# Merge steps of a two-layer graph network: two steps' chunks in one word, and products of 96 columns

## The chip, the cores and the metric

One core of a Trainium2 chip runs the kernel. The metric is device time in microseconds (us), the median of several runs of the whole program; lower is better. In the rows below PE is TensorE's matmul, PEld its weight load, DVE is VectorE, ACT is ScalarE, POOL is GpSimd and SP is SyncE, whose work here is to issue DMAs. A q behind an engine's name is its instruction queue.

## What is computed

The inputs are 100,000 nodes of 96 f32 features, 50,000 edges sorted by destination, with 32 features each, and the weights of two layers:

```python
def _egnn_conv(x, src, dst, edge_attr, W_msg, W_edge, W_root, b):
    msg = x[src] @ W_msg + edge_attr @ W_edge
    agg = segment_max(msg, dst, num_segments=x.shape[0])
    agg = where(isneginf(agg), 0.0, agg)
    return agg + x @ W_root + b
c1 = leaky_relu(_egnn_conv(X, ..., W1_msg, W1_edge, W1_root, b1))
c2 = leaky_relu(_egnn_conv(c1, ..., W2_msg, W2_edge, W2_root, b2))
return layernorm(x + c2)
```

## The kernel before, in words

The program runs four phases: an edge phase and a merge for each of the two layers (the merges are called A and B in the prediction).

**Edge phase** (98 groups of 512 edges). GpSimd gathers source rows (L397), TensorE turns them (L443), multiplies by the message and edge weights (L450), VectorE scans along the edges for the running maximum of each destination (L866), TensorE turns the result back (L460), and VectorE copies it into the tensor `hold` (L873): 391 chunks of 128 edges by 96 columns, which stay in SBUF. Beside this TensorE computes the root term x @ W_root + b of all nodes (L473, L482), which goes to DRAM. In the edge phase of layer 1 the tables of the merge are worked out from the destinations: TensorE counts (L499 to L508), and VectorE writes them in small pieces, one per edge group (L764 to L840). `piece_words` (L821 to L823) makes `step_words`, one 32-bit word per merge step, which holds the place of the step's chunk in `hold`. The one-hot matrices, which both merges use, are also written once to DRAM as bytes (L884 to L887, stores at L277).

**Merge** (L558 to L571). The nodes lie in 782 blocks of 128. A merge step adds what one chunk of edges gives to one block: a matmul of a one-hot matrix (128 edges to 128 nodes, the weights) with the chunk (the moving operand) into the block's slot in PSUM. Chunks and blocks are walked together, in 391 + 782 - 1 = 1172 steps. A step moves on either to the next chunk or to the next block, and which of the two is known only from the data. So TensorE's queue reads the words into registers (L554) and works out two addresses per step: of the chunk in `hold` (word times 4, plus a base) and of the slot in PSUM (word times BACK, plus a constant of the step, modulo the 16,384 bytes of a partition, plus a base). These register operations are packed into one instruction per step, which the rows list as FUSED_REGOPS. An f32 matmul is issued as two passes, each with its weight load.

Steps go in 147 batches of 8. Sixteen words (two batches) are loaded at a time. The loop of TensorE's queue:

```python
if k % 2 == 0:
    words = load_words(k * BATCH, min(2 * BATCH, TP - k * BATCH))
pe.wait_ge(made if layer == 0 else grown, k + 1)
for i in range(n):
    ...
    nc.tensor.matmul(...).then_inc(stepped[layer], 1)
```

The one-hots of a batch lie in one of two buffers (`onehot`, NS = 2). In merge A VectorE makes them (L914 to L919), waiting for the steps of the batch before last; in merge B GpSimd loads their bytes from DRAM (L412) and casts them to f32 in four pieces (L430). ScalarE copies finished blocks out of PSUM (L684), seeds freed slots with the root term (L670), and SyncE's queue stores results and loads root rows (L307 to L336). Where ScalarE may go on, it learns from counts of steps that it loads four at a time into registers, followed by one `max` per word (L708 to L715), two of them in the last load of a layer.

In merge B each table of 2048 nodes (49 tables) is finished as soon as its blocks are out: VectorE applies the leaky ReLU (L932), adds x (L935), takes the statistics of the layer norm (L937 to L951) and normalises part of the blocks (L955); ScalarE takes the root of the variance (L719) and normalises the rest (L725). ScalarE issues its copies, seeds, roots and normalisations in one written order (L691 to L706).

Of the kernel before, what the change touches and what calls it, by code (L numbers as in the profile page):

```python
# [5 lines left out]
F32 = mybir.dt.float32  # L6
BF16 = mybir.dt.bfloat16
I32 = mybir.dt.int32
U8 = mybir.dt.uint8
# [8 lines left out]
C = 4  # L18
# [8 lines left out]
RING = 8  # L27
NS = 2
# [9 lines left out]
TABLES_TAKE = 3  # L38


def gnn(nc, x, src, dst, edge_attr, weights, out):
# [27 lines left out]
    with ExitStack() as ctx:  # L69
        def sb(name, shape, dt):  # L70
            return ctx.enter_context(nc.sbuf_tensor(name, shape, dt))
# [21 lines left out]
        hold_all = sb("hold", [P, CH * D + P - D], F32)  # L93
        arena = sb("arena", [P, max(2 * UNIT_RING * UB * D + (EDGE_RING + 4) * GE + 2 * BATCH * P // 4, UNIT_RING * UB * D + 5 * RI * D)], F32)
        onehot = sb("onehot", [P, NS, BATCH, P], F32)
        keep = sb("keep", [P, EDGE_RING, GE], BF16)
        assert EDGE_RING == 4
# [9 lines left out]
        rows = sb("rows", [ROWS_ON + 1, TP], I32)  # L107
# [21 lines left out]
        ring_bytes = keep[:].rearrange("p i n -> p (i n)").bitcast(U8).rearrange("p (i n) -> p i n", n=BW)  # L129
# [6 lines left out]
        flat = hold_all[:]  # L136
# [3 lines left out]
        def scratch(n, dt=F32):  # L140
            free_at[0] -= n
            a = flat[:, free_at[0]:free_at[0] + n]
            return a if dt is F32 else a.bitcast(dt)
# [17 lines left out]
        place_row = scratch(TP)  # L161
        end_row, open_row, open_i = scratch(2 * NSB), scratch(NBATCH), scratch(NBATCH, I32)
# [10 lines left out]
        BACK = next(b for b in range(RING * C * SLOT) if (b * D + SLOT) % (RING * C * SLOT) == 0)  # L173
# [66 lines left out]
        def within(value, most):  # L240
            return nc.s_assert_within(value, 0, most, skip_runtime_bounds_check_because="a place in the merge, worked out on the chip from counts of chunks")
# [194 lines left out]
        def _(pe):  # L436
# [116 lines left out]
            def load_words(at, n):  # L553
                return nc.values_load_multi_w_load_instructions(  # L554
                    step_words[0:1, at:at + n], engines=[mybir.EngineType.PE], min_val=0, max_val=(CH - 1) * D,
                    skip_runtime_bounds_check_because="places in the merge, worked out on the chip from counts of chunks")[1]

            def merge(layer):  # L558
                for k in range(NBATCH):
                    n = min(BATCH, T - k * BATCH)  # L560
                    if k % 2 == 0:
                        words = load_words(k * BATCH, min(2 * BATCH, TP - k * BATCH))
                    if layer == 0:
                        pe.wait_ge(made, k + 1)
                    else:
                        pe.wait_ge(grown, k + 1)
                    for i in range(n):
                        word = words[k % 2 * BATCH + i]
                        chunk_at, place_at = word, within((word * BACK + (k * BATCH + i) * SLOT) % (RING * C * SLOT), (RING * C - 1) * SLOT)
                        nc.tensor.matmul(ps_bytes[:, bass.ds(place_at, SLOT)].bitcast(F32), onehot[:, k % NS, i, :], flat[:, bass.ds(chunk_at, P)],  # L570
                                         start=False, stop=True, skip_group_check=True).then_inc(stepped[layer], 1)  # L571
# [163 lines left out]
        def _(dve):  # L735
# [13 lines left out]
            def then(ins):  # L749

                link[0] += 1
                ins.then_inc(vec, 1)
                dve.wait_ge(vec, link[0])
# [67 lines left out]
            def piece_words():  # L821
                nc.vector.tensor_scalar(step_words, chunk_row[0:1, :], float(D), None, ALU.mult)
                then(nc.vector.tensor_tensor(place_row[0:1, :], steps_f[0:1, :], chunk_row[0:1, :], ALU.subtract))  # L823
# [168 lines left out]
```

## Time and profile before

| | |
|---|---|
| median of 3 runs | 1884.19 us |
| lowest and highest run | 1880.46 and 1887.78 us |
| profiled execution, span from first to last instruction | 1876.7 us |
| TensorE busy in matmuls | 1519.6 us (81%) |
| VectorE busy | 1313.2 us (70%) |
| ScalarE and GpSimd busy | 1080.4 and 1084.8 us (58% each) |
| mean granted TensorE clock | 0.950 |

The times are of the whole program on the device. The profile is of one execution; what lies before its first and after its last instruction is not in the span, and its own total is not listed apart from the runs. A share of busy time is a mean over phases with different limits, so the rows are best read phase by phase. The phases: edge phase 1 up to about 549 us, merge A from 549 to 871, edge phase 2 to 1382, merge B with the finishes to the end.

### The profile page before, as it was taken

Reading aid. Unit: us, or ns where it says so; the run is one execution under the profiler, and the core shown is the slowest. Engines: PE = TensorE matmul, PEld = TensorE weight load, DVE = VectorE, ACT = ScalarE, POOL = GpSimd, SP = SyncE. Lnnn points to the kernel's source line nnn. Section 1 sums busy time; section 2 is a strip of 40 time slices with the busy share of each in tenths; the row PEclk is TensorE's granted clock in tenths of the full one; section 3 lists DMA queues with packets and bytes.
Section 4 is the critical chain, followed back from the end, with each engine's and each line's share of the span. In section 5 each row is a group of like instructions: output and inputs, shape, how many; then the busy total and the mean of one; then the engine's idle time right before and its main releaser. Section 6 shows DMA issues by size and latency. Waiting matters only on the chain.

```text
span 1876.7 us, 37108 instructions
## 1 busy us (share of the span) xinstructions
PE 1519.6 (81%) x11422; PEld 1348.9 (72%) x11422; DVE 1313.2 (70%) x2383; ACT 1080.4 (58%) x2450; POOL 1084.8 (58%) x1454
## 2 busy tenths in 40 slices
PE   3998888988889888886889888988987767676763
PEld 3677777777778888885778777777777667666662
DVE  3677676777665555553667767677736899999998
ACT  2354444545443455553555555555535888888887
POOL 6777777767600000002777777777757787675663
PEclk9999999999999999998999999999998998988887
DMA  7779999999865777885788888888867899999996
GB/s 145 203 213 266 271 266 263 264 276 273 245 226 169 226 248 261 279 277 189 204 225 228 238 229 235 226 223 242 223 223 215 267 290 298 296 299 296 294 300 176
DMA packets 505022, 459.13 MB, mean 245 GB/s; under 512 B 348553, under 2 KB 412340, under 8 KB 504836
## 3 DMA queue, kind: packets, MB, share of 16 engines
q1 hardware_dynamic: 444118, 321.15, 59.9%
q0 software_dynamic: 30976, 57.72, 12.7%
q10 hardware_dynamic: 29742, 77.88, 10.6%
q8 instruction: 103, 1.69, 0.4%
q14 instruction: 83, 0.68, 0.1%
HBM read 283.25 MB, written 173.37 MB: 243 GB/s over the span
## 4 chain that ended last, share of the span: by engine, by line
PE 30%; DVE 25%; DMA 19%; POOL 15%; issue 9%; ACT 1%; SPq 1%; POOLq 0%; DVEq 0%; ACTq 0%
PE ps L570 18%; DMA onehot_bytes<-arena 14%; POOL arena L397 13%; DVE stats L937 6%; DVE arena L880 4%; DMA arena<-nodes,src_perm 4%; DVE arena L935 4%; DVE arena L932 4%; PE ps L482 4%; POOL onehot L430 2%; PE ps L450 2%; PE ps L473 2%; PE ps L443 2%; DVE arena L955 2%; DVE arena L866 1%
## 5 line engine op out<-in xcount | busy, mean ns | idle before, releaser
L570 PE MATMUL ps<-hold,onehot 128*128 x4688 | 612.7, 293 | 186.2 <-POOL onehot L430 139.5
L570 PEld LDWEIGHTS ps<-hold,onehot 128*128 128x128 f32 x4688 | 582.3, 205 | 217.0 <-issue 216.8
L397 POOL DMA_INDIRECT arena<-nodes,src_perm x392 | 370.0, 944 | 473.4 <-SPq L364 354.2
L482 PEld LDWEIGHTS ps<-w_root,onehot 97*128 97x128 f32 x3136 | 400.9, 194 | 99.7 <-issue 97.5
L397 POOL DMA_INDIRECT arena<-in_x_dram,src_all x392 | 374.4, 955 | 143.0 <-issue 114.3
L482 PE MATMUL ps<-w_root,onehot 97*128 97x128 f32 x3136 | 417.6, 277 | 0.0
L430 POOL CAST onehot<-keep 128x256 f32<-128x256 uint8 x588 | 298.8, 556 | 115.5 <-PE ps L570 72.4
L634 ACT COPY arena<-ps 128x384 f32<-128x384 f32 x392 | 187.5, 478 | 274.2 <-PE ps L482 272.4
L684 ACT COPY arena<-ps 128x384 f32<-128x384 f32 x392 | 166.6, 477 | 208.6 <-PE ps L570 208.5
L866 DVE TENSOR_TENSOR_SCAN arena<-keep,arena,ps 96x512 f32<-96x512 bf16 x196 | 247.7, 1264 | 46.6 <-PE ps L450 46.2
L880 DVE TENSOR_TENSOR onehot<-count,rel 128x1024 f32<-128x1024 bf16 x147 | 179.5, 1222 | 142.3 <-PE ps L570 141.2
L880 DVE TENSOR_TENSOR arena<-ps,rel 128x1024 uint8<-128x1024 f32 x147 | 175.5, 1216 | 110.6 <-DMA onehot_bytes<-arena 110.4
L473 PE MATMUL ps<-ident,arena 128*96 128x128 f32 x1568 | 240.9, 277 | 0.0
L725 ACT ACTIVATE arena<-arena,small 128x96 f32<-128x96 f32 x635 | 232.7, 454 | 1.6 <-DVE small L951 1.6
L450 PE MATMUL ps<-arena,w_edge 128*96 128x512 f32 x392 | 207.2, 611 | 0.0
L443 PE MATMUL ps<-ident,arena 128*128 128x128 f32 (+1 forms) x784 | 125.7, 284 | 96.2 <-DMA arena<-nodes,src_perm 63.7
L670 ACT COPY ps<-arena 128x384 f32<-128x384 f32 x392 | 175.9, 488 | 8.8 <-DMA arena<-root 8.3
L473 PEld LDWEIGHTS ps<-ident,arena 128*96 128x96 f32 x1568 | 177.2, 128 | 2.8 <-issue 2.4
L851 DVE TENSOR_TENSOR arena<-ps,arena 128x512 f32<-128x512 f32 x98 | 67.6, 690 | 146.9 <-ACT arena L613 144.5
L443 PEld LDWEIGHTS ps<-ident,arena 128*128 128x128 f32 (+1 forms) x784 | 93.2, 146 | 106.9 <-DMA arena<-nodes,src_perm 61.4
L624 ACT COPY onehot<-ps 96x512 f32<-96x512 f32 x196 | 114.3, 583 | 95.1 <-PE ps L473 92.4
L460 PE MATMUL ps<-ident,arena 96*128 96x96 f32 (+1 forms) x782 | 99.0, 249 | 52.8 <-DVE arena L880 51.8
(97 smaller groups left out, 1158.4 us busy)
## 6 DMA issues: line engine op xcount, KB each, us to landing
root<-arena ACTq DMA_DIRECT2D x196, 384.0 KB
arena<-root SPq DMA_DIRECT2D x196, 384.0 KB, 4.4
nodes<-arena SPq DMA_DIRECT2D x98, 384.0 KB, 2.7
arena<-nodes SPq DMA_DIRECT2D x98, 384.0 KB
arena<-in_x_dram SPq DMA_DIRECT2D x97, 384.0 KB
arena<-in_x_dram SPq DMA_DIRECT2D x48, 768.0 KB, 8.0
out_dram<-arena SPq DMA_DIRECT2D x48, 768.0 KB, 4.6
onehot_bytes<-arena SPq DMA_DIRECT2D x147, 128.0 KB
```

The source lines that it names most:

```text
L397: nc.gpsimd.indirect_dma_start(out=gathered[t.ring][0:t.p, i, 0:D], out_offset=None, in_=table_in, in_offset=bass.IndirectOffsetOnAxis(ap= ...
L430: last = nc.gpsimd.tensor_copy(onehot[:, k % NS, i:i + PIECE, :].rearrange("p t n -> p (t n)"), bytes_back(k, 1)[:, 0, i * P:(i + PIECE) * P])
L443: last = nc.tensor.transpose(et_ps[:, r:t.cols:C], gathered[t.ring][0:t.p, r, :], ident[0:t.p, 0:t.p])
L450: nc.tensor.matmul(em_ps[t.b2][0:D, 0:t.cols], w_edge[:, t.layer, :], edges_t[t.b2][:, 0:t.cols], start=True, stop=True).then_inc(em_full, 1)
L473: last = nc.tensor.transpose(nt_ps[m % 2][0:D, to], node_in[u % UNIT_RING][:, at:at + D], ident[:])
L482: last = nc.tensor.matmul(no_ps[m % 2][:, i * P:(i + 1) * P], nodes_t[m % NODE_RING][0:D + 1, i * P:(i + 1) * P], w_root[0:D + 1, layer * ...
L570: nc.tensor.matmul(ps_bytes[:, bass.ds(place_at, SLOT)].bitcast(F32), onehot[:, k % NS, i, :], flat[:, bass.ds(chunk_at, P)], start=False, ...
L634: nc.scalar.copy(root_out[u % UNIT_RING][:, at:at + C * D].rearrange("p (j d) -> p j d", d=D), no_ps[m % 2].rearrange("p (j k) -> p j k", ...
L670: nc.scalar.copy(slot[:, n % RING, :, 0:D], root_in[u % UNIT_RING][:, at:at + C * D].rearrange("p (j d) -> p j d", d=D),).then_inc(seeded[ ...
L725: last = nc.scalar.activation(nodes_out[s % 3][:, at], nodes_out[s % 3][:, at], ACT.Identity, bias=small[:, 5 + 2 * (s % 2), j:j + 1], sca ...
L866: nc.vector.tensor_tensor_scan(msgs[t.b2][0:D, at], keep[0:D, t.ring, at], em_ps[t.b2][0:D, at], msgs[1 - t.b2][0:D, GE - 1:GE], ALU.min, ...
L880: return nc.vector.tensor_tensor(to[:, 0:n, :], row.rearrange("p (a n) -> p a n", a=1).broadcast_to([P, n, P]), rel[:, k * BATCH:k * BATCH ...
```

## The change

The chunk index of a step, plus the distance of the step from the end of its round of 32 (`ahead`), takes ten bits. Two steps' values go into one 32-bit word, so that 16 loaded words serve 32 steps, and `load_words` runs every fourth batch (LOADED = 4). A step takes its half out of the word (`% SECOND` for even steps, `// SECOND` for odd ones), multiplies by the 384 bytes of a chunk and has the chunk's address; the slot follows from the same product (times BACK, now 84, modulo 16,384), with no constant of the step. For the chunk's address to hold `ahead`, the data before `hold` must belong to the same tensor: the buffers `onehot` and `keep` (together RING * C * D words per partition) now lie at its head. The product takes the 96 columns of the chunk in place of 128 (96 and 32 of what follows). `piece_words` has five VectorE operations in place of two. The number of steps, batches, buffers, semaphores, waits and DMAs is as before.

```diff
+SECOND = 1 << 10
+LOADED = 4
...
-        hold_all = sb("hold", [P, CH * D + P - D], F32)
+        AHEAD = RING * C * D
+        hold_all = sb("hold", [P, AHEAD + CH * D + P - D], F32)
...
-        onehot = sb("onehot", [P, NS, BATCH, P], F32)
-        keep = sb("keep", [P, EDGE_RING, GE], BF16)
-        assert EDGE_RING == 4
+        assert EDGE_RING == 4 and AHEAD == NS * BATCH * P + EDGE_RING * GE // 2
+        onehot = hold_all[:, 0:NS * BATCH * P].rearrange("p (s t n) -> p s t n", s=NS, n=P)
+        keep = hold_all[:, NS * BATCH * P:AHEAD].bitcast(BF16).rearrange("p (i n) -> p i n", n=GE)
...
-        rows = sb("rows", [ROWS_ON + 1, TP], I32)
+        rows = sb("rows", [ROWS_ON + 1, TP // 2], I32)
...
-        flat = hold_all[:]
+        flat = hold_all[:, AHEAD:]
...
+        ahead_i, ahead_row = scratch(TP, I32), scratch(TP)
...
-        BACK = next(b for b in range(RING * C * SLOT) if (b * D + SLOT) % (RING * C * SLOT) == 0)
+        hold_bytes, CHUNK = hold_all[:].bitcast(U8), 4 * D
+        BACK = next(b for b in range(RING * C * SLOT) if (b * CHUNK + SLOT) % (RING * C * SLOT) == 0)
+        assert CH + RING * C < SECOND and (CH + RING * C) * SECOND < 1 << 24 and T % 2 == 0 and BATCH % 2 == 0
+
+        def ahead(t):
+
+            return RING * C - t % (RING * C)
+
+        def chunk_view(t, word):
+
+            at, most = 4 * AHEAD - ahead(t) * CHUNK, (CH - 1 + ahead(t)) * CHUNK
+            return hold_bytes[:, at:at + most + CHUNK][:, bass.ds(within(word, most), CHUNK)].bitcast(F32)
...
                 for k in range(NBATCH):
                     n = min(BATCH, T - k * BATCH)
-                    if k % 2 == 0:
-                        words = load_words(k * BATCH, min(2 * BATCH, TP - k * BATCH))
+                    if k % LOADED == 0:
+                        words = load_words(k * BATCH // 2, min(LOADED * BATCH, TP - k * BATCH) // 2)
...
                     for i in range(n):
-                        word = words[k % 2 * BATCH + i]
-                        chunk_at, place_at = word, within((word * BACK + (k * BATCH + i) * SLOT) % (RING * C * SLOT), (RING * C - 1) * SLOT)
-                        nc.tensor.matmul(ps_bytes[:, bass.ds(place_at, SLOT)].bitcast(F32), onehot[:, k % NS, i, :], flat[:, bass.ds(chunk_at, P)],
+                        word = words[(k % LOADED * BATCH + i) // 2]
+                        chunk_at = pe.snap((word // SECOND if i % 2 else word % SECOND) * CHUNK)
+                        place_at = within(chunk_at * BACK % (RING * C * SLOT), (RING * C - 1) * SLOT)
+                        nc.tensor.matmul(ps_bytes[:, bass.ds(place_at, CHUNK)].bitcast(F32), onehot[:, k % NS, i, :], chunk_view(k * BATCH + i, chunk_at),
                                          start=False, stop=True, skip_group_check=True).then_inc(stepped[layer], 1)
...
             def piece_words():
-                nc.vector.tensor_scalar(step_words, chunk_row[0:1, :], float(D), None, ALU.mult)
-                then(nc.vector.tensor_tensor(place_row[0:1, :], steps_f[0:1, :], chunk_row[0:1, :], ALU.subtract))
+                pairs = lambda a: a[0:1, :].rearrange("a (t n) -> a t n", n=2)
+                nc.vector.tensor_tensor(place_row[0:1, :], steps_f[0:1, :], chunk_row[0:1, :], ALU.subtract)
+                then(nc.vector.tensor_scalar(ahead_i[0:1, :], steps_i[0:1, :], RING * C - 1, None, ALU.bitwise_and))
+                then(nc.vector.tensor_scalar(ahead_row[0:1, :], ahead_i[0:1, :], -1.0, float(RING * C), ALU.mult, ALU.add))
+                then(nc.vector.tensor_tensor(ahead_row[0:1, :], ahead_row[0:1, :], chunk_row[0:1, :], ALU.add))
+                nc.vector.scalar_tensor_tensor(step_words, pairs(ahead_row)[:, :, 1], float(SECOND), pairs(ahead_row)[:, :, 0], ALU.mult, ALU.add)
```

## Rows read from the trace of the kernel before

**Rows 1.** The page: span, and the chain that ended last, by line.

```profile
span 1876.7 us, 37108 instructions
...
PE ps L570 18%; DMA onehot_bytes<-arena 14%; POOL arena L397 13%; DVE stats L937 6%; DVE arena L880 4%; DMA arena<-nodes,src_perm 4%; DVE arena L935 4%; DVE arena L932 4%; PE ps L482 4%; POOL onehot L430 2%; PE ps L450 2%; PE ps L473 2%; PE ps L443 2%; DVE arena L955 2%; DVE arena L866 1%
```

**Rows 2.** By stage: length, busy us of PE, PEld, DVE, ACT, POOL; clock; DMA.

```profile
549.20:870.75 321.55, 282.36 (x2344) 268.81 (x2344) 178.09 (x146) 160.18 (x387) 0.00 (x0) 0.99 0.73 239
...
1487.00:1876.70 389.70, 251.25 (x1758) 238.33 (x1757) 356.33 (x1132) 338.01 (x917) 254.06 (x489) 0.86 0.95 282
```

**Rows 3.** Who waited for whom, 549 to 870 us: total us, times, longest.

```profile
ACT arena L684 <- PE ps L570: 158.0, 97, 9.2
DVE onehot L880 <- PE ps L570: 141.2, 145, 2.5
...
PE ps L570 <- issue: 39.0, 71, 1.2
...
PE ps L570 <- DVE onehot L880: 2.1, 1, 2.1
```

**Rows 4.** Merge matmuls 653 to 663 us (timeline); line views of L570 and L554.

```profile
653.42 3.83 PE L570 MATMUL ps<-hold,onehot 128*128 x32 [0.66 <-issue]
657.91 3.83 PE L570 MATMUL ps<-hold,onehot 128*128 x32 [0.65 <-issue]
...
653.42 2.05 PE L570 MATMUL ps<-hold,onehot 128*128 x16 [0.66 <-issue]
...
L570 PE MATMUL ps<-hold,onehot x24: 275/275/372, 653.4 to 656.1; 128*128 x24
L570 PEldq FUSED_REGOPS  x16: 102/103/103, 653.3 to 656.0; - x16
...
L554 PEldq TENSOR_LOAD <-rows x73: 862/1268/1870, 552.1 to 868.5; - x73
```

**Rows 5.** Busy time of L570 alone, from the second load of merge A on.

```profile
553.20:870.75 317.55, 278.39 (x2325) 264.84 (x2324) 1.00 0.73 237
```

**Rows 6.** Who waited for whom, 1382 to 1487 us.

```profile
DVE arena L932 <- ACT arena L684: 25.7, 1, 25.7
PE ps L570 <- POOL onehot L430: 25.3, 14, 3.5
```

**Rows 7.** Weight loads after a stall (L570), and transposes of 96 columns (L460).

```profile
653.42 0.30 PEld L570 LDWEIGHTS ps<-hold,onehot 128*128 128x128 f32 x2 [0.84 <-issue]
...
L570 PEld LDWEIGHTS ps<-hold,onehot x2: 186/188/189, 653.4 to 653.5; 128*128 128x128 f32 x2
...
1111.60 0.49 PE L460 MATMUL ps<-ident,arena 96*128 96x96 f32 x4
...
L460 PEld LDWEIGHTS ps<-ident,arena x4: 139/140/143, 1111.5 to 1111.8; 96*128 96x128 f32 x4
```

**Rows 8.** ScalarE's register instructions at L714: four operations, and the last with two.

```profile
L714 ACTq FUSED_REGOPS  x1: 55/55/55, 642.3 to 642.3; - x1
...
L714 ACTq FUSED_REGOPS  x1: 43/43/43, 867.1 to 867.1; - x1
```

**Rows 9.** VectorE's one-hots, 655 to 659 us (timeline).

```profile
655.58 1.22 DVE L880 TENSOR_TENSOR onehot<-count,rel 128x1024 f32<-128x1024 bf16 x1 [1.48 <-PE ps L570]
```

**Rows 10.** Busy time by stage, a stretch late in merge A.

```profile
820.00:840.00 20.00, 16.75 (x141) 15.82 (x140) 11.07 (x10) 11.82 (x29) 0.00 (x0) 1.00 0.88 280
```

**Rows 11.** GpSimd's casts, 1416 to 1426 us (timeline).

```profile
1419.21 1.43 POOL L430 CAST onehot<-keep 128x256 f32<-128x256 uint8 x4 [0.19 <-PE ps L570]
1420.86 4.33 POOL L430 CAST onehot<-keep 128x256 f32<-128x256 uint8 x4 [0.21 <-PE ps L570]
```

**Rows 12.** VectorE around the table of words, 98 to 106 us (timeline).

```profile
99.94 0.75 DVE L822 TENSOR_SCALAR rows<-hold 1x1176 int32<-1x1176 f32 x1
100.62 1.37 DVE L823 TENSOR_TENSOR hold<-hold 1x1176 f32<-1x1176 f32 x1
102.02 1.28 DVE L866 TENSOR_TENSOR_SCAN arena<-keep,arena,ps 96x512 f32<-96x512 bf16 x1
```

More of the change, by code:

```diff
@@ L128, in gnn @@
         BW = BATCH * P
-        ring_bytes = keep[:].rearrange("p i n -> p (i n)").bitcast(U8).rearrange("p (i n) -> p i n", n=BW)
+        ring_bytes = hold_all[:, NS * BATCH * P:AHEAD].bitcast(U8).rearrange("p (i n) -> p i n", n=BW)
         bytes_out = arena[:, at_rest + 4 * GE:at_rest + 4 * GE + 2 * BW // 4].bitcast(U8).rearrange("p (i n) -> p i n", n=BW)
@@ L554, in load_words @@
                 return nc.values_load_multi_w_load_instructions(
-                    step_words[0:1, at:at + n], engines=[mybir.EngineType.PE], min_val=0, max_val=(CH - 1) * D,
+                    step_words[0:1, at:at + n], engines=[mybir.EngineType.PE], min_val=0, max_val=(CH + RING * C) * SECOND - 1,
                     skip_runtime_bounds_check_because="places in the merge, worked out on the chip from counts of chunks")[1]
```

## Prediction

> **What bounds the kernel now.** I read the page first: the span and the chain that ended last, in which many lines share and the largest piece, 18%, is the line of the merge matmul [rows 1]. So the next view is the busy time by stage [rows 2]: the reader should see that the merge of layer 1 (merge A) is 321.6 us in which TensorE is busy 282.4, and that the end of merge B (from 1487 us) belongs to VectorE, busy 356 of 389.7. The change also touches, through a table, a few us of the first edge phase.
>
> In merge A ScalarE waits 158.0 us and VectorE 141.2 us for the matmuls, and TensorE has hardly a wait for them (2.1 us once) but 39.0 us of "issue" in 71 pieces [rows 3]. So TensorE and its own instruction queue bound it. One period shows how [rows 4]: 32 passes (16 steps of two passes each, since an f32 matmul goes as two) run in one burst of 3.83 us, and the next burst starts 4.49 us after the first. Between bursts the queue loads 16 words into registers; that load takes 1.27 us in the median. Inside a burst the first 16 passes take 2.05 us; the last of them lasts 0.275, and the first lasts 0.372 and not 0.275 because of the stall, so 15 distances make (2.05 − 0.275 − 0.097)/15 = 0.112 us a pass, 0.223 a step. The queue itself would be faster: its 16 register instructions start at 653.3 to 656.0, 2.7/15 = 0.18 us a step, of which the register instruction is 0.103.
>
> From this comes the price of one load. Over 317.55 us there are 2325 passes [rows 5]; 2325 × 0.1115 = 259.2 us, so 58.3 us are left for 73 loads: 0.80 us each. A load of 1.27 costs only 0.80 because the queue had run ahead. I count a load of 1.27 us plus 0.04 of restart, less the lead, so the mean lead was 0.51.
>
> Merge B is another matter: in its first 105 us, up to 1487, TensorE waits 25.3 us for GpSimd's casts, and VectorE's finishes wait 25.7 us for the first table of nodes [rows 6]. After that VectorE is busy almost without pause with the finishes [rows 2]: TensorE's speed there costs nothing.
>
> **The change, part by part.**
>
> *Fewer loads.* Words are now loaded every fourth batch, still 16 at a time: 37 loads a merge in place of 74. The duration of a load I leave at 1.27, since its 16 words are the same.
>
> *Narrower products.* Moving 96 columns for 128 would take a pass from 0.112 to 0.084 if columns alone counted. They don't: after a stall the first pass lasts 372 ns and not 275 [rows 4], 97 more, because it waits for its weights, and the two weight loads there are 0.30 − 0.189 = 0.11 us apart with nothing else in their way [rows 7]. That is the rate at which 128 f32 columns go in, and the change leaves the weights alone. Passes of 96 columns exist too: four take 0.49 us [rows 7], where four of 128 would take 3 × 0.112 + 0.275 = 0.61, so 0.03 less each, or 0.082 a pass. But those are transposes whose weight load lasts 139 to 143 ns, not 186 to 189, so they do not prove the faster rate here. I take 0.108 a pass, 0.216 a step, near the rate of the weight loads; the ends are 0.164 a step (columns alone) and 0.223 (nothing).
> By the Trainium skill (TensorE: Matmul & The Clock Gate, section "Back-to-back issue gap") the gap of isolated matmuls grows with the moving columns alone; it adds that in a stream the weight load counts as well. By the first half of that rule the sum would be that of the first rival below; the rows at the stall speak against it.
>
> *Register work of a step.* By the code a step needs six register operations now: two multiplications, three additions and a mod. Afterwards six: a division or a mod to take the chunk out of the word, two multiplications, a mod, two additions; the constant per step has moved into the word. So an addition becomes a second mod or a division. ScalarE's register instruction of four simple operations takes 55 ns and of two 43 [rows 8]: 6 ns an operation and 31 for the instruction. Six of those are 67, so 36 of the 103 belong to multiplying and to the mod. The new operation then adds 0 to 36 ns: the queue's step becomes 0.181 to 0.217. No row divides them further, so I take the middle, 0.199, and keep both ends.
>
> *The one-hots are late next.* Each batch of eight steps needs a one-hot made by VectorE in the buffer of the batch before last. The last pass of a batch started at 653.42 + 2.05 − 0.275 = 655.20; the one-hot started at 655.58 and took 1.22 [rows 4, 9]. With 0.04 to TensorE's queue, 0.15 of register and issue and 0.11 for the weights, the first product of the batch after next can start 1.90 us after that last pass. Today it is due 17 passes later, 1.90 us: just in time, and each load has hidden it. With passes of 0.108 it is due at 1.84, so it is 0.07 late once in four batches, and the queue loses its lead at the third and fourth batch. The lead at the next load is then what eight steps gain: 8 × (0.216 − 0.199) = 0.14.
>
> *Sum for merge A, per 32 steps.* Now 2 × (16 × 0.223 + 0.80) = 8.74 us. After: 32 × 0.216 + 0.07 + 1.31 − 0.14 = 8.15. Gain 0.59, times 1172/32 = 36.6: 21.5 us. With a queue step of 0.181 it is 26.6, with 0.217 (then the queue sets the step) 15.1, with passes unchanged 17.
>
> *Who else must keep pace.* ScalarE waits for the merge, not the merge for it [rows 3]. The DMA engines are 88% busy late in merge A [rows 10]; 7% more pace gives 94%. I add nothing.
>
> *Merge B.* In its first 105 us some 18 loads become 9, which by the above would free 9 × 0.8 = 7 us, but GpSimd is late next: four casts take 1.4 us when free and 4.3 beside VectorE's long operations [rows 11]. I take 4 us, between 0 and 7. After 1487 us nothing.
>
> *The table of words.* VectorE's two operations on 1176 elements (0.75 and 1.37 us) become five: the subtraction (1.37), a bit operation (some 0.75), a multiply-add (0.75), an addition (1.37), and a packing of half the length (0.7): 3 us more, estimated from the two rows. The scan behind them starts at 102.02, right when they end [rows 12], and the scans hold TensorE up, so nothing covers it: I take 3 us on the path, bounds 0 (if the edge phase catches up) and 3.1.
>
> *One tensor for two buffers and the waiting data.* No instruction is added or taken away and no wait changes; nothing is behind it that could be uncovered. Zero.
>
> Total: −21.5 − 4 + 3 = −22.5 us. The profiled execution has a span of 1876.7 us; the runs shown have a median of 1884.2, 7.5 above it, and I put the difference on that: **1862 us**. Its own range, with the ends of the queue's step, of merge B and of the table: 1852 to 1874.
>
> **The rivals.**
>
> *Columns alone count.* Passes fall to 0.082, the queue sets the step: 32 × 0.199 + 1.31 = 7.68, 38.7 us less in merge A, 6 in merge B, 3 for the table: 1842. For it: the transposes of 96 columns [rows 7]. Against it: the weight loads at the stall. Chance 0.13.
>
> *The register work eats the gain.* If the extraction costs more than any row here shows, the queue has no lead and sets the step: 32 s + 1.31 equals today's 8.74 at s = 0.232, a register instruction of 154 ns. At 0.225 merge A gains 8, merge B 1, less 3: 1878, no change that a measurement can tell. Chance 0.14.
>
> *Slower by the same place.* If a step's operations don't fit one instruction, a second one comes to it, which costs at least the 43 ns of the shortest and an issue of its own: s = 0.25. Then 32 × 0.25 + 1.31 = 9.31, 21 us more in merge A, 4 in merge B, 3 for the table: 1912. It decides from s = 0.232 upward. For it: 103 ns is already over half of the queue's step [rows 4], and its reserve to the step of TensorE is 0.04 us. Against it: the number of operations is the same. Chance 0.11.
>
> *The change does less than it says*: each load grows as its words serve more steps. The words per load are the same 16, so I give this 0.02, at 1876 to 1884.
>
> **How the numbers follow.** The forecast has 0.60. About 0.5% (9.4 us) is what a measurement of this kernel can tell from no change. Faster by more than that: the forecast and the first rival, less a tail: 0.73. Within it: 0.16. Slower: 0.11. The range from 1840 to 1884 takes in the first two rivals and leaves out the slower one and a little of the fast end.
>
> **What would show it.** In the changed profile: 37 loads of about 1.27 us a merge (74 in all); bursts of 64 passes with one gap of 1.0 to 1.2 us; passes 0.108 apart inside a burst (0.082 speaks for the first rival, 0.112 for no gain from columns); a register instruction of 103 to 139 ns, one per step (two per step or over 154 ns speaks for the slower rival); merge A some 300 us long in place of 321.6; the stage up to 549.2 about 3 us longer; VectorE still busy without a pause from about 1480 us. The forecast is wrong if merge A is shorter than 280 or longer than 312 us, or if its time comes back in the later stages.

## The result, and the profile after

| | before | after |
|---|---|---|
| median | 1883.70 us (4 runs) | 1910.18 us (4 runs) |
| lowest and highest run | 1880.46 and 1887.78 us | 1905.17 and 1913.95 us |
| profiled execution, span | 1876.7 us | 1906.2 us (its own time 1908.06 us) |

The ratio is 1.0144 with a 95% interval of 1.0110 to 1.0178: the change costs about 26 us. The forecast was 1862 us.

The page of the changed kernel: span, granted clock in 40 slices, chain that ended last by line ([rows 1] of before). The merge matmul is now L586, the cast L445, and the one-hots carry the name `hold`, since they lie in that tensor.

```profile
span 1906.2 us, 37037 instructions
...
PEclk9999999999999999888999999999987787887886
...
PE ps L586 23%; POOL arena L412 17%; DMA onehot_bytes<-arena 13%; POOL hold L445 7%; DVE arena L900 4%; DMA arena<-nodes,src_perm 3%; PE ps L497 3%; DVE stats L957 3%; DVE arena L955 2%; DVE arena L952 2%; PE ps L488 1%; DVE arena L886 1%; PE ps L465 1%; PE ps L458 1%; DMA hold<-onehot_bytes 1%
```

The merge matmul grew from 18% of the chain to 23%, and the clock line has 7 and 8 where merge B runs. By stage, with the stages cut at the first and the last product of each merge (columns as in [rows 2]; the seventh value is the granted clock): merge A, the first 100 us of merge B, and all of merge B.

```profile
552.70:885.30 332.60, 289.64 (x2344) 283.90 (x2344) 178.02 (x146) 159.89 (x386) 0.00 (x0) 0.94 0.70 231
1401.60:1501.60 100.00, 79.25 (x524) 76.04 (x524) 48.50 (x157) 48.60 (x127) 71.64 (x145) 0.81 0.72 220
1401.60:1885.50 483.90, 364.17 (x2343) 349.98 (x2344) 398.60 (x1268) 383.54 (x1035) 346.43 (x652) 0.81 0.91 273
```

The same cuts of the kernel before.

```profile
549.20:870.40 321.20, 282.02 (x2343) 268.67 (x2344) 178.09 (x146) 160.18 (x387) 0.00 (x0) 0.99 0.73 239
1382.10:1482.10 100.00, 75.65 (x561) 71.92 (x561) 55.34 (x169) 55.97 (x148) 76.63 (x153) 0.91 0.75 229
1382.10:1854.80 472.70, 330.02 (x2343) 313.37 (x2344) 400.46 (x1268) 382.32 (x1032) 334.58 (x652) 0.88 0.93 278
```

So the start of merge A is 3.5 us later, merge A 11.4 us longer, the edge phase of layer 2 4.6 us longer (885.3 to 1401.6 against 870.4 to 1382.1), merge B 11.2 us longer, and what follows the last product 1.2 us shorter. The granted clock has two levels in these records, 1.0 (2.4 GHz) and 0.5 (1.2 GHz), so a mean of g means that 2 × (1 − g) of the stretch was at 1.2 GHz. Added up from the single records of the clock, these are 38 us of merge A in place of 3, and 186 us of merge B in place of 110.

Inside merge A, first two bursts of the timeline ([rows 4] of before).

```profile
638.12 7.38 PE L586 MATMUL ps<-hold 128*128 x64 [0.91 <-issue]
646.59 7.44 PE L586 MATMUL ps<-hold 128*128 x64 [1.09 <-issue]
```

Then the line views (ns, shortest/median/longest): the loads of merge A, products and register instructions of both merges, and the register instructions that follow one load.

```profile
L569 PEldq TENSOR_LOAD <-rows x37: 950/1170/2746, 550.0 to 879.6; - x37
...
L586 PE MATMUL ps<-hold x4688: 274/276/525, 552.7 to 1885.5; 128*128 x196
L586 PEldq FUSED_REGOPS  x2344: 126/134/154, 552.5 to 1884.1; - x196
...
L586 PEldq FUSED_REGOPS  x7: 128/128/137, 646.4 to 647.7; - x7
```

Bursts of 64 passes with one load each, and one register instruction per step, as forecast. But a burst at full clock lasts 7.38 to 7.44 us: (7.4 − 0.275 − 0.1)/63 = 0.112 a pass, as before. And the register instruction takes 126 to 139 ns (one came to 154) in place of 103; while the queue runs freely, the starts of these instructions lie 0.209 and 0.217 us apart in turn, 0.213 a step in place of 0.181.

Who waited for whom in merge A ([rows 3] of before; us, times, longest).

```profile
ACT arena L700 <- PE ps L586: 170.4, 97, 10.4
DVE hold L900 <- PE ps L586: 141.5, 140, 4.1
...
PE ps L586 <- issue: 24.1, 24, 2.5
PE ps L586 <- DVE hold L900: 20.8, 13, 2.0
```

The two waits of TensorE sum to 44.9 us (before 41.1) although there are half as many: 37 of 1.2 us in place of 72 of 0.57. Thirteen of them now end with a one-hot.

And where the clock falls: two bursts of the timeline.

```profile
672.32 7.44 PE L586 MATMUL ps<-hold 128*128 x64 [1.18 <-issue]
681.16 9.08 PE L586 MATMUL ps<-hold 128*128 x64 [1.40 <-DVE hold L900]
```

The merge's own busy time in two stretches around the fall (PE, PEld, then the granted clock).

```profile
672.80:683.00 10.20, 8.80 (x78) 8.64 (x78) 1.00 0.71 233
683.00:686.40 3.40, 3.40 (x18) 3.40 (x18) 0.50 0.69 231
```

The second burst contains 3.4 us at 0.5, which 18 passes touch. In it 16 passes start, 0.213 us apart; at 0.112 there would have been 30. What TensorE did before the fall: a burst, a pause of 1.40 us, and 2 us of the next burst. Merge A has eight such falls, beside the one at its start which before has too.

### The profile page after: what moved, and what is told of

Same layout as the page of the kernel before. It is cut to its first block, busy times and chain, and to the rows that moved or that the text cites. A ratio compares the mean times of both kernels' runs of the same rounds, so it can differ in the third digit from the quotient of the medians.

```text
span 1906.2 us, 37037 instructions
## 1 busy us (share of the span) xinstructions
PE 1567.7 (82%) x11422; PEld 1407.4 (74%) x11422; DVE 1313.2 (69%) x2386; ACT 1081.2 (57%) x2450; POOL 1097.2 (58%) x1454
## 4 chain that ended last, share of the span: by engine, by line
PE 31%; POOL 24%; DMA 18%; DVE 15%; issue 10%; SPq 1%; ACT 1%; POOLq 0%; DVEq 0%; ACTq 0%
PE ps L586 23%; POOL arena L412 17%; DMA onehot_bytes<-arena 13%; POOL hold L445 7%; DVE arena L900 4%; DMA arena<-nodes,src_perm 3%; PE ps L497 3%; DVE stats L957 3%; DVE arena L955 2%; DVE arena L952 2%; PE ps L488 1%; DVE arena L886 1%; PE ps L465 1%; PE ps L458 1%; DMA hold<-onehot_bytes 1%
## 5 line engine op out<-in xcount | busy, mean ns | idle before, releaser
L586 PE MATMUL ps<-hold 128*128 x4688 | 654.4, 308 | 166.9 <-POOL hold L445 120.2
L586 PEld LDWEIGHTS ps<-hold 128*128 128x128 f32 x4688 | 634.1, 221 | 187.7 <-issue 186.6
L497 PEld LDWEIGHTS ps<-w_root,hold 97*128 97x128 f32 x3136 | 403.1, 195 | 99.8 <-issue 97.1
L497 PE MATMUL ps<-w_root,hold 97*128 97x128 f32 x3136 | 420.2, 278 | 0.0
L445 POOL CAST hold<-hold 128x256 f32<-128x256 uint8 x588 | 310.6, 575 | 114.9 <-PE ps L586 83.6
L900 DVE TENSOR_TENSOR hold<-count,rel 128x1024 f32<-128x1024 bf16 x147 | 179.5, 1222 | 154.2 <-PE ps L586 141.5
L886 DVE TENSOR_TENSOR_SCAN arena<-hold,arena,ps 96x512 f32<-96x512 bf16 x196 | 247.8, 1264 | 49.8 <-PE ps L465 49.5
L640 ACT COPY hold<-ps 96x512 f32<-96x512 f32 x196 | 114.2, 583 | 91.9 <-PE ps L488 85.2
```

The lines of the kernel that those rows point to most:

```text
L445: last = nc.gpsimd.tensor_copy(onehot[:, k % NS, i:i + PIECE, :].rearrange("p t n -> p (t n)"), bytes_back(k, 1)[:, 0, i * P:(i + PIECE) * P])
L497: last = nc.tensor.matmul(no_ps[m % 2][:, i * P:(i + 1) * P], nodes_t[m % NODE_RING][0:D + 1, i * P:(i + 1) * P], w_root[0:D + 1, layer * ...
L586: nc.tensor.matmul(ps_bytes[:, bass.ds(place_at, CHUNK)].bitcast(F32), onehot[:, k % NS, i, :], chunk_view(k * BATCH + i, chunk_at), start ...
L886: nc.vector.tensor_tensor_scan(msgs[t.b2][0:D, at], keep[0:D, t.ring, at], em_ps[t.b2][0:D, at], msgs[1 - t.b2][0:D, GE - 1:GE], ALU.min, ...
L900: return nc.vector.tensor_tensor(to[:, 0:n, :], row.rearrange("p (a n) -> p a n", a=1).broadcast_to([P, n, P]), rel[:, k * BATCH:k * BATCH ...
```

## The experiments

Each kernel ran beside runs of the kernel before on the same chip; a ratio is to those. Stage lengths are of one profiled execution. Single runs of the kernel before lay between 1870.6 and 1904.6 us, so a few us in one stage of one execution say little by themselves. This holds for merge B above all: the kernel before with halved one-hots, below, has no edit in merge B, and yet its merge B took 491.9 us at a granted 0.86 in the profiled execution, its longest run, where before has 472.7. Merge A of the same two took 320.9 and 321.2.

### The change cut in two

First the change with its old width: words packed, products of 128 columns.

```diff
-            return hold_bytes[:, at:at + most + CHUNK][:, bass.ds(within(word, most), CHUNK)].bitcast(F32)
+            return hold_bytes[:, at:at + most + SLOT][:, bass.ds(within(word, most), SLOT)].bitcast(F32)
...
-                        nc.tensor.matmul(ps_bytes[:, bass.ds(place_at, CHUNK)].bitcast(F32), onehot[:, k % NS, i, :], chunk_view(k * BATCH + i, chunk_at),
+                        nc.tensor.matmul(ps_bytes[:, bass.ds(place_at, SLOT)].bitcast(F32), onehot[:, k % NS, i, :], chunk_view(k * BATCH + i, chunk_at),
```

> The changed kernel with products of 128 columns again; packed words, register work and loads stay as changed. The changed kernel's batches at full clock are 16 us faster over merge A, but merge A has 34 us at the low clock where before had none after its start. Theory C (columns): narrower products leave TensorE less active, and with pauses that lowers its granted clock. Then the low clock goes from merge A, merge A takes 303 to 312 us (332.6 in the changed kernel, 321.2 before) and the total is 1868 to 1882. Theory G (gaps): the longer pause at each load (1.1 to 2.5 us where it was 0.5 to 1.2), since the queue has lost its lead, lowers the clock. Then the low clock stays, merge A takes 325 to 335 us and the total is 1903 to 1914.

Then the kernel before with nothing but the narrow product.

```diff
-                        nc.tensor.matmul(ps_bytes[:, bass.ds(place_at, SLOT)].bitcast(F32), onehot[:, k % NS, i, :], flat[:, bass.ds(chunk_at, P)],
+                        nc.tensor.matmul(ps_bytes[:, bass.ds(place_at, 4 * D)].bitcast(F32), onehot[:, k % NS, i, :], flat[:, bass.ds(chunk_at, D)],
```

> The kernel before with products of 96 columns and nothing else. Theory C: merge A gets stretches at the low clock, takes 325 to 340 us, the first 100 us of merge B get longer too, and the total is 1895 to 1912. Theory G: pauses are as before, the clock stays at full in merge A, merge A takes 317 to 323 us and the total is 1879 to 1887. If columns alone set a pass (the first rival of the prediction), passes fall to 0.082 us and merge A is under 300; the changed kernel's passes of 0.112 speak against that already.

Packed and wide: 1885.76 us (10 runs), ratio 1.0019 (0.9985 to 1.0052): no change. Narrow alone: 1896.76 us (10 runs), 1.0069 (1.0041 to 1.0097): 13 us slower. Packed and wide by stage: merge A, the first 100 us of merge B, and all of it.

```profile
549.50:871.20 321.70, 277.58 (x2343) 270.83 (x2344) 178.05 (x146) 160.95 (x388) 0.00 (x0) 0.99 0.73 238
1383.20:1483.20 100.00, 76.35 (x531) 72.70 (x532) 48.71 (x158) 49.81 (x131) 71.76 (x146) 0.86 0.74 226
1383.20:1861.50 478.30, 331.14 (x2343) 314.77 (x2344) 397.98 (x1265) 381.69 (x1030) 339.94 (x653) 0.89 0.92 275
```

Its loads in merge A, from the second on:

```profile
L569 PEldq TENSOR_LOAD <-rows x36: 873/1382/2517, 558.7 to 865.6; - x36
```

Two of its bursts at nearly the place where the clock of the changed kernel fell:

```profile
678.96 7.51 PE L586 MATMUL ps<-hold 128*128 x64 [1.49 <-DVE hold L900]
688.10 7.44 PE L586 MATMUL ps<-hold 128*128 x64 [1.63 <-DVE hold L900]
```

Narrow alone, merges A and B:

```profile
546.80:869.30 322.50, 281.48 (x2344) 270.05 (x2344) 178.04 (x146) 160.08 (x387) 0.00 (x0) 0.99 0.73 238
...
1381.00:1875.80 494.80, 373.15 (x2344) 359.82 (x2344) 400.13 (x1269) 386.05 (x1042) 352.86 (x652) 0.78 0.90 267
```

Its products:

```profile
L570 PE MATMUL ps<-hold,onehot x4688: 274/275/525, 546.8 to 1875.7; 128*128 x196
```

Three things follow. First, fewer columns buy nothing: merge A is as long with 96 as with 128, and a product's record has the same 275 ns. Second, fewer columns cost clock. In merge A it takes both halves of the change: the wide kernel has pauses of 1.49 and 1.63 us and its bursts stay at 7.5 us (after the merge's start one fall in all of merge A, where the changed kernel has eight), the narrow one with its short pauses has 0.99 too, and only narrow products with long pauses fall to 0.94. In merge B, whose products also wait for GpSimd's casts, narrow products alone take the clock from 0.88 to 0.78 in these two executions, and the stage is 22 us longer; over the runs the whole is 13 us longer. The clock doesn't rest on two executions: its mean over the whole program was 0.912 to 0.929 in the ten runs of the narrow kernel, and 0.945 to 0.958 in the 19 of the kernel before beside them. So theory C was right about the clock of the wide kernel and the total of the narrow one, but not about the wide kernel's time, nor about merge A of the narrow kernel. Third, the packing was to bring 17 us in merge A even with unchanged passes, and brought none; that needs its own experiments.

By the Trainium skill (TensorE: Matmul & The Clock Gate, section "A second HAM failure mode: psum-queue depth-cycling") short idle times between groups of matmuls made the clock gate oscillate in one kernel. The changed kernel fits that (0.94 with pauses over 1 us); the packed and wide one, with the same pauses, stayed at 0.99, so here the pauses were not enough by themselves.

### Short pauses in place of long ones

The changed kernel with four words loaded before every batch, with either width (the wide one has the edit of the product as well).

```diff
-LOADED = 4
+LOADED = 1
```

> Packed words and register work as changed, products of 128 columns, but four words (eight steps) loaded before every batch in place of sixteen before every fourth. Theory L (lead): the pause of a load is its duration less what the queue has run ahead; with a register instruction of 0.134 us the queue gains only 0.01 us a step, so sixteen words cost 1.36 us once where two loads cost 0.70 each. ScalarE's loads of four words take 0.306 us, so a batch costs the queue 8 x 0.212 + 0.35 = 2.05 us: merge A 297 to 308 us without low clock, total 1860 to 1874. Rival F (a fixed price per load, whatever its words): 147 loads at 0.7 us or more, merge A over 360 us, total over 1920.

> The same with products of 96 columns, that is, the changed kernel with four words loaded before every batch. Theory: in merge A the low clock needs both, narrow products and pauses of over a microsecond; with pauses of 0.3 us it is gone there (under 10 us of low clock, 38 in the changed kernel), merge A takes 297 to 310 us. In merge B the pauses come from GpSimd's casts, so there the narrow products still bring low clock and cost 10 to 20 us against the run with 128 columns: total 1874 to 1892. If narrow products alone lower the clock, merge A is over 315 us and the total over 1890.

Wide 1894.84 us (10 runs), ratio 1.0050 (1.0019 to 1.0081); narrow 1907.86 us (6 runs), 1.0096 (1.0063 to 1.0130). The wide one: its loads in merge A.

```profile
L569 PEldq TENSOR_LOAD <-rows x146: 327/333/859, 555.2 to 883.0; - x146
```

Its merges A and B:

```profile
553.50:884.40 330.90, 304.16 (x2343) 277.44 (x2344) 178.06 (x146) 159.90 (x386) 0.00 (x0) 0.99 0.71 232
1395.80:1871.00 475.20, 337.02 (x2343) 314.16 (x2344) 399.10 (x1268) 382.99 (x1035) 341.91 (x656) 0.90 0.93 278
```

The narrow one, merges A and B.

```profile
561.20:891.70 330.50, 299.16 (x2344) 276.44 (x2344) 178.04 (x146) 160.79 (x388) 0.00 (x0) 0.99 0.72 233
1403.70:1895.20 491.50, 371.75 (x2343) 354.27 (x2344) 399.58 (x1269) 384.68 (x1040) 338.44 (x656) 0.80 0.90 270
```

The expected gain did not come: I had taken 0.306 us for a load of four words, and over the merge they took 0.44 in the mean (0.33 in the median). Eight steps then cost the queue 8 × 0.213 + 0.44 + about 0.1 for the restart = 2.24 us, and 330.9 us over 146.5 batches is 2.26: the queue, not TensorE, sets this kernel. For the clock the pair is clean. With short pauses the narrow products keep it in merge A (0.99) and the two merges A are equally long, so a merge A of over 315 us is not the sign of a low clock that I had made it. In merge B the narrow kernel has 0.80 against 0.90 and is 16 us longer in these executions; over the runs the whole is 13 us slower, as it was without the packing.

### The price of the register work alone

The wide kernel with one step's value per word, taken out by a mod: the register work of the change with the loads of before.

```diff
-LOADED = 4
+LOADED = 2
...
-                        words = load_words(k * BATCH // 2, min(LOADED * BATCH, TP - k * BATCH) // 2)
+                        words = load_words(k * BATCH, min(LOADED * BATCH, TP - k * BATCH))
...
-                        word = words[(k % LOADED * BATCH + i) // 2]
-                        chunk_at = pe.snap((word // SECOND if i % 2 else word % SECOND) * CHUNK)
+                        word = words[k % LOADED * BATCH + i]
+                        chunk_at = pe.snap((word % SECOND) * CHUNK)
...
-                nc.vector.scalar_tensor_tensor(step_words, pairs(ahead_row)[:, :, 1], float(SECOND), pairs(ahead_row)[:, :, 0], ALU.mult, ALU.add)
+                nc.vector.tensor_copy(step_words, ahead_row[0:1, :])
```

> One word per step as before (sixteen loaded for sixteen steps) and products of 128 columns, but the register work of the changed kernel's even steps: mod, multiplication, addition, multiplication, mod, addition. It holds the cost of the register work by itself. Theory L: the register instruction takes 0.126 to 0.139 us, the lead per load falls from 0.65 to about 0.2 us, each of 73 pauses grows from 0.70 to 1.1 to 1.2 us, merge A takes 340 to 352 us (321 before), the total is 1903 to 1920. Rival H: the register work hides beside the matmuls, since 0.21 is under the 0.2235 of a step: merge A 319 to 326 us, total 1882 to 1892.

1912.62 us (4 runs), ratio 1.0142 (1.0086 to 1.0198). Its register instructions:

```profile
L586 PEldq FUSED_REGOPS  x2344: 124/127/153, 549.5 to 1882.0; - x196
```

Its merge A:

```profile
549.70:899.50 349.80, 282.17 (x2343) 268.80 (x2344) 178.07 (x146) 160.28 (x387) 0.00 (x0) 1.00 0.68 220
```

At full clock the register work, with one mod more, lengthens merge A by 28.6 us, and halving the loads then gives that back (349.8 to 321.7). Both parts of the packing are real and they cancel.

Why 24 ns in an instruction that ran beside the passes cost so much is seen in the pauses. I added up every distance between two product starts of merge A above 0.23 us, less a pass. Beside it stands what a load should cost by a simple rule: its duration, plus 0.04 for the restart, less the lead, which is the steps that the queue ran freely times what it gains on TensorE in each (0.2235 less its own step).

| kernel | load, mean us | queue's step | free steps | pause by the rule | pause measured |
|---|---|---|---|---|---|
| before | 1.31 | 0.181 | 16 | 0.67 | 0.70 (73, sum 50.9) |
| one value per word | 1.32 | 0.205 | 16 | 1.06 | 1.09 (73, sum 79.6) |
| packed, wide | 1.47 | 0.213 | 8 | 1.43 | 1.39 (36, sum 50.0) |
| after | 1.42 | 0.213 | 8 | 1.38 | 1.36 (36, sum 48.8) |

(0.205 is 0.181 with 24 ns more; the 8 are the two batches before the load less what the late one-hots take away, as the prediction assumed.) In the two packed rows the rule is a fit, since the trace shows other parts: after a load has started, TensorE still starts passes for 0.70 us in the kernel before, 0.35 with one value per word, 0.21 packed and wide, and 0.18 after. This is the lead, and it shrinks as said, but the restart takes 0.10 to 0.13 and not 0.04. Load plus restart less this lead gives 0.71, 1.10, 1.40 and 1.36. Half the loads at twice the price are the same 50 us.

### Register work that doesn't pack

To take the register work back I wrote the mods and the division as bit operations, with either width.

```diff
-                        chunk_at = pe.snap((word // SECOND if i % 2 else word % SECOND) * CHUNK)
-                        place_at = within(chunk_at * BACK % (RING * C * SLOT), (RING * C - 1) * SLOT)
+                        chunk_at = pe.snap((word >> 10 if i % 2 else word & (SECOND - 1)) * CHUNK)
+                        place_at = within((chunk_at * BACK) & (RING * C * SLOT - 1), (RING * C - 1) * SLOT)
```

> The changed kernel with a shift and bit masks in place of the division and the two mods of a step; products stay at 96 columns. Both theories: the register instruction falls from 126 to 139 ns to about 80, and the queue regains its lead, so the pause per load falls below 0.9 us. Theory G: with the short pauses the clock stays at full, merge A takes 288 to 300 us, the total is 1858 to 1872. Theory C: the clock still falls, merge A takes 300 to 322 us, and the total is 1880 to 1900.

> Shift and masks as in the run before, and products of 128 columns: packed words and halved loads alone remain of the change. Both theories expect the clock at full in merge A, merge A of 288 to 300 us, and a total of 1858 to 1872. If stretches of low clock remain there, neither holds, and the halved loads themselves (longer bursts, other pauses) are to blame.

2231.99 and 2228.96 us (4 runs each), ratios 1.1866 (1.1806 to 1.1927) and 1.1852 (1.1792 to 1.1912). The narrow one's register instructions:

```profile
L586 PEldq FUSED_REGOPS  x4688: 46/76/97, 556.6 to 2213.6; - x196
...
L586 PEldq ALU_OP  x3516: 32/32/42, 556.5 to 2213.5; - x196
```

A long stretch of its merge A:

```profile
600.00:1100.00 500.00, 464.46 (x2081) 452.02 (x2081) 159.27 (x130) 150.53 (x364) 0.00 (x0) 0.51 0.44 142
```

The wide one, the same stretch:

```profile
600.00:1100.00 500.00, 454.22 (x2082) 339.91 (x2082) 158.62 (x130) 150.02 (x363) 0.00 (x0) 0.90 0.44 141
```

My expectation failed: a bit operation stands as an instruction of its own (ALU_OP) and cuts the packed one, so a step has 2 packed and 1.5 single instructions in place of one. This is the mechanism of the slower rival, at its true price: merge A took 561.2 us, and outside the loads its steps follow each other on the queue at 0.43 us in the mean. The pair shows two things more. At a granted 0.51 and at 0.90 the same stretch holds 2081 and 2082 passes: where the queue is the bound, as here, the clock costs nothing. And since the queue sets the same pace in both, the columns are all that differs between 0.51 and 0.90.

### The one-hots

Thirteen pauses of the changed kernel end with a one-hot. In the wide kernel I had VectorE make each batch's one-hot in two halves of four steps, each released and awaited by itself; the control is the same edit in the kernel before.

```diff
+HALF = 4
...
-                    if layer == 0:
-                        pe.wait_ge(made, k + 1)
...
+                        if layer == 0 and i % HALF == 0:
+                            pe.wait_ge(made, 2 * k + i // HALF + 1)
...
-                    if k >= NS:
-                        dve.wait_ge(stepped[0], BATCH * (k - NS + 1))
-                    compare(onehot[:, k % NS, :, :], k, count[:]).then_inc(made, 1)
+                    for i in range(0, min(BATCH, T - k * BATCH), HALF):
+                        if k >= NS:
+                            dve.wait_ge(stepped[0], BATCH * (k - NS) + i + HALF)
+                        compare(onehot[:, k % NS, :, :], k, count[:], i, HALF).then_inc(made, 1)
```

> The changed kernel with products of 128 columns, and in merge A the one-hots of a batch made in two halves of four steps, each as soon as the four steps before last in the same buffer are done. What it tells apart: whether the queue loses its lead in the third and fourth batch of a load because it has to wait for a one-hot that comes just in time. If so, it can run ahead 32 x (0.2235 - 0.2125) = 0.35 us over a load, the pause falls from 1.36 to 1.0 to 1.15 us, merge A to 306 to 316 us (321.7 with whole one-hots), the total to 1868 to 1880. If the lead is not lost there, merge A stays at 319 to 324 us and the total at 1882 to 1890.

> The kernel before with one-hots in halves, as a control. With a load every second batch the pause itself gives VectorE the time, so the one-hots are never late there: merge A 318 to 323 us, total within 5 us of the kernel before. If halves are worth something by themselves, it gets faster by as much as the run beside it.

With the packing 1878.02 us (12 runs), ratio 0.9980 (0.9957 to 1.0003); in the kernel before 1879.14 us (13 runs), 0.9987 (0.9963 to 1.0011). Packed, wide and halved, merge A:

```profile
548.10:863.20 315.10, 275.49 (x2343) 269.15 (x2344) 201.15 (x292) 160.52 (x388) 0.00 (x0) 0.99 0.74 244
```

TensorE's waits in it:

```profile
PE ps L587 <- DVE hold L902: 33.4, 30, 1.8
PE ps L587 <- issue: 8.0, 5, 2.7
```

The kernel before with halves, merge A:

```profile
553.30:874.20 320.90, 282.68 (x2344) 269.63 (x2344) 201.31 (x292) 160.97 (x388) 0.00 (x0) 0.99 0.74 240
```

Merge A of the packed kernel falls from 321.7 to 315.1 us, that of before stays (320.9 against 321.2). So the late one-hots were a small part of the missing gain, 6 to 7 us. The pauses fell only to 1.30 in the mean, not to the 1.0 to 1.15 that I expected, though the lead, read as above, rose from 0.21 to 0.34 us, near the 0.35 that I had worked out: it had been larger than I thought, and the restart longer. This is the best version found; its interval takes in 1, so it is not shown to beat the kernel before. A repeat of the changed kernel came in at 1909.55 us (4 runs), 1.0103 (1.0056 to 1.0151):

> The changed kernel once more, on the chip of these runs: all theories 1904 to 1916 us, merge A 328 to 336 us with 25 to 45 us at the low clock. If it comes within 5 us of the kernel before, the low clock was a matter of that chip and not of the kernel.

Its merge A took 333.2 us at 0.95, with 36 us at the low clock, so that the loss and the low clock came again.

## Why the prediction was wrong, point by point

**The granted clock, which the prediction never mentioned, is the missing step.** The rows that it rested on show the clock at 0.99 in merge A and 0.86 from 1487 us on, and I read past them. Packed kernels differ by 24 us between 128 and 96 columns (1885.76 and 1910.18), unpacked ones by 13. The mean clock of every single run agrees: with the packing 0.913 to 0.932 in the narrow kernels and 0.943 to 0.958 in the wide ones. So of the 48 us between the forecast (1862) and the result, 24 are the price of the narrow products, and the other 24 a gain of the packing that did not come. In the profiled executions 10.9 us of the first 24 are merge A (321.7 to 332.6). They lie in the passes: the distances of up to 0.23 us between two starts sum to 278.9 us, in the wide kernel to 267.4, while the pauses sum to 48.8 and 50.0. Merge B is 5.6 us longer in the one comparison (478.3, 483.9), 16 and 22 in the others, single executions all.

**Narrower products: term mis-sized.** I took 0.108 a pass between 0.082 and 0.112; it is 0.112, so the end called "nothing" was right, 8.2 us over 1172 steps. By the Trainium skill (TensorE: Matmul & The Clock Gate, section "Back-to-back issue gap") the spacing in a stream of weight loads and matmuls is set by both; the merge fits that, with 0.112 for 96 and for 128 columns under the same 128 columns of weights.

**Register work: the value within its ends, the consequence too small.** One instruction per step, as said. It took 134 ns in the median where I took 121, near the upper end of 139, and the queue's step became 0.213 where I took 0.199.

**Fewer loads: price mis-sized.** I had 1.17 us for a pause (1.27 for the load and 0.04 for the restart, less a lead of 0.14); it was 1.39 in the wide kernel, since the load took 1.47 in the mean (before 1.31; I had taken the median) and the restart 0.13, while the lead was 0.21: 36 × 0.22 = 8 us. What made loads longer wasn't isolated. And I forgot a term: my 0.80 per load of before held 7.4 us of small delays between passes (58.3 less the 50.9 of the pauses), which stay (10.6 in the wide kernel, the start of the merge at the low clock included) and which I had let vanish but for 0.07 a period, 2.6 us in all: 8 us more. The three sum to 24 of the 23.4 us between the forecast for merge A (36.6 × 8.15 = 298.3) and the wide kernel's 321.7. So without the narrow products the result would have been no change. (The ends that the prediction names for its own range add up to 1851 and 1872 us, not 1852 and 1874; nothing hangs on it.)

**The one-hots** were late next, as said; with halves they gave 6 to 7 us back.

**Merge B**: "After 1487 us nothing" was wrong, since TensorE's speed there does reach the end. VectorE waits for the roots of ScalarE (L719), which stand in ScalarE's written order behind the copies of finished blocks (L684), and those wait for the merge's products. The waits from the first product of merge B on, in the kernel before and in the narrow one:

```profile
DVE small L950 <- ACT small L719: 38.8, 49, 6.7
ACT arena L684 <- PE ps L570: 49.4, 16, 10.8
...
DVE small L950 <- ACT small L719: 61.2, 49, 8.4
ACT arena L684 <- PE ps L570: 78.4, 27, 10.6
```

VectorE's wait for the roots is 22.4 us longer, and merge B 22.1. In all ten executions without bit operations merge B less this wait is 431 to 435 us. That the copies are what makes the roots late is read from the written order and from both waits growing together; no run has another order.

The 4 us that I expected can't be read from single executions, in which merge B moved by 19 us without an edit. The medians, less the difference in merge A, leave +1.2 us for the wide kernel, −0.6 with four words and −1.3 with halves, where my −4 and the table's +3 make −1. So the gain is not shown, and not excluded.

**The word table**: five operations on VectorE as priced,

```profile
100.90 1.36 DVE L839 TENSOR_TENSOR hold<-hold 1x1176 f32<-1x1176 f32 x1
102.19 0.76 DVE L840 TENSOR_SCALAR hold<-hold 1x1176 int32<-1x1176 int32 x1
102.98 0.76 DVE L841 TENSOR_SCALAR hold<-hold 1x1176 f32<-1x1176 int32 x1
103.78 1.37 DVE L842 TENSOR_TENSOR hold<-hold 1x1176 f32<-1x1176 f32 x1
105.19 0.76 DVE L843 SCALAR_TENSOR_TENSOR rows<-hold 1x588 int32<-1x588 f32 x1
```

5.0 us in place of 2.1 [rows 12], so 2.9 more where I had 3. Merge A began 3.5 us later, but over the runs its start moved between 548.1 and 561.2 us with this table and 546.8 and 553.3 with the old one, so that the 3 us reach the path is not shown. The 4.6 us of the edge phase of layer 2 did not come again: 511.3 us in the repeat, 511.7 before.

**The rivals.** The slower one had nearly the measured time (1912), but by luck: its mechanism, a register instruction of 154 ns or two per step, did not occur. Its price was shown by the bit operations. "The register work eats the gain" came nearest in substance: at the wide kernel's 1885.76 us it is what happened, with a register instruction of 134 ns where I had put its turning point at 154, because the gain was smaller than the sum said. The queue did not come to set the step, though (0.213 us against 0.2235); its lead shrank.

## What to carry to other kernels

A wait that is partly hidden has a price of its length less the lead of the queue that runs into it. Before trading work between the waits and that queue, work out the lead from the queue's own step: halving the waits while slowing the queue can leave the sum as it was. An engine that is busy almost without pause can still be made to wait by a slower one, through the written order of a third. And read the granted clock of a stage beside its busy time: an edit that makes TensorE's work lighter without making its passes shorter can cost clock, and only a version with that edit alone shows it.

## What the runs showed of the hardware that was not expected

- Products of 96 columns in place of 128, with no other edit, kept their 0.112 us a pass at full clock and took the granted clock of merge B from 0.88 to 0.78, and the whole from 1884.06 to 1896.76 us. At one pace, set by the queue, products of 128 columns had a granted 0.90 over 500 us and those of 96 had 0.51.
- At 1.2 GHz the passes started 0.213 us apart, at 2.4 GHz 0.112.
- TensorE's register arithmetic packs multiplications, additions, mods and divisions into one instruction per step. Steps with a second mod take 124 to 131 ns and those with a division 134 to 139, against 103 with an addition; `&` and `>>` aren't packed, 32 ns each as an instruction of their own, and a step of the queue became 0.43 us long.
- A load of 4 words into TensorE's registers took 0.33 us in the median and up to 0.86, one of 16 words 0.87 to 2.5 (the two wide kernels). Per word there is little to gain from loading more at a time: 0.08 against 0.09 us in the medians, 0.11 against 0.09 in the means.
